# Two attention blocks with normalised queries and keys: score matmuls of two key heads on halves of the array's rows

## What is computed

```python
def _qk_norm(a):
    var = jnp.mean(jnp.square(a), axis=-1, keepdims=True)
    return a * jax.lax.rsqrt(var + EPS)

def _attn(xq, xkv, wq, wk, wv, wo, rep):
    q = jnp.einsum('btc,chd->bthd', xq, wq)      # 16 query heads of 64
    k = jnp.einsum('btc,chd->bthd', xkv, wk)     # 4 key heads of 64
    v = jnp.einsum('btc,chd->bthd', xkv, wv)
    q, k = (_qk_norm(q), _qk_norm(k))
    k = jnp.repeat(k, rep, axis=2)               # rep = 4
    v = jnp.repeat(v, rep, axis=2)
    logits = jnp.einsum('bqhd,bkhd->bhqk', q, k) * (1.0 / np.sqrt(64))
    attn = jax.nn.softmax(logits, axis=-1)
    out = jnp.einsum('bhqk,bkhd->bqhd', attn, v)
    return out.reshape(B, Tq, H * Dh) @ wo

x = _rmsnorm(latents, s1)
latents = latents + _attn(x, inputs, wq_c, wk_c, wv_c, wo_c, rep)   # block L2_ca
latents = latents + _swiglu_ffn(_rmsnorm(latents, s2), w1_1, w2_1)
z = _rmsnorm(latents, s3)
latents = latents + _attn(z, z, wq_s, wk_s, wv_s, wo_s, rep)        # block L2_sa
```

## Time and profile before

| what | value |
|---|---|
| median of 3 runs | 2165.87 us (2164.4 to 2177.83) |
| profiled execution, its own time | 2163.83 us |
| span of its trace, first to last instruction | 2162.0 us |
| mean granted TensorE clock | 0.921 of full |
| instructions | 34309 |

### The profile page before, as it was taken

How to read it: one execution, slowest core, us unless ns; L and a number is a source line. 1 busy time by engine, 2 the same in 40 slices (tenths; PEclk the granted TensorE clock), 3 DMA queues, 4 the chain that set the end, 5 groups by cost and what they waited for, 6 DMA issues and landing times.

```text
span 2162.0 us, 34309 instructions
## 1 busy us (share of the span) xinstructions
PE 1812.8 (84%) x10658; PEld 1289.2 (60%) x10658; DVE 1326.3 (61%) x3343; ACT 866.9 (40%) x2497; POOL 641.2 (30%) x710
## 2 busy tenths in 40 slices
PE   5969998389938689999869999695886969999888
PEld 4747775278837576776755554483443835555457
DVE  5856666111148765666757667595776956656555
ACT  4635554022216425555324444242331434545421
POOL 2325554200032334555500000040000415455433
PEclk9979998599969889999979999797998979999979
DMA  4000000378830000010100010101001000001100
GB/s 165 29 21 16 15 0 1 117 248 301 284 131 1 0 0 23 15 46 0 64 9 13 15 65 0 49 1 59 0 0 53 18 0 12 21 10 29 50 1 17
DMA packets 34247, 102.76 MB, mean 48 GB/s; under 512 B 2624, under 2 KB 25696, under 8 KB 26976
## 3 DMA queue, kind: packets, MB, share of 16 engines
q1 hardware_dynamic: 32608, 97.79, 13.1%
q0 software_dynamic: 1536, 3.67, 0.5%
HBM read 93.20 MB, written 8.26 MB: 47 GB/s over the span
## 4 chain that ended last, share of the span: by engine, by line
PE 55%; issue 15%; DVE 13%; POOL 8%; ACT 4%; DMA 3%; SPq 0%; POOLq 0%; DVEq 0%; ACTq 0%
PE ps L909 8%; PE ps L792 7%; POOL arena L1786 6%; PE ps L732 4%; PE ps L944 4%; PE ps L805 4%; PE ps L737 3%; PE ps L855 3%; PE ps L787 3%; PE ps L837 3%; PE ps L1039 2%; PE ps L1023 2%; DMA arena<-rows_hbm 2%; PE ps L832 2%; PE ps L724 2%
## 5 line engine op out<-in xcount | busy, mean ns | idle before, releaser
L1786 POOL TENSOR_TENSOR arena<-arena,rinv 112x375 f32<-112x375 f32 (+1 forms) x448 | 371.4, 829 | 524.5 <-DVE rinv L1460 513.6
L805 PEld LDWEIGHTS ps<-cst,arena 112*125 112x125 f32 (+1 forms) x1408 | 206.1, 182 | 182.5 <-POOL arena L1786 81.2
L792 PE MATMUL ps<-arena 128*112 128x112 f32 (+1 forms) x1024 | 277.3, 385 | 14.6 <-ACT arena L1148 13.0
L805 PE MATMUL ps<-cst,arena 112*125 112x112 f32 (+1 forms) x1408 | 237.7, 281 | 57.0 <-POOL arena L1786 56.7
L1148 ACT ACTIVATE arena<-ps,negmax 112x375 f32<-112x375 f32 (+1 forms) x384 | 190.5, 501 | 188.1 <-DVE negmax L1455 187.2
L1455 DVE TENSOR_REDUCE negmax<-ps 112x1 f32<-112x375 f32 (+1 forms) x288 | 159.4, 553 | 157.9 <-PE ps L792 157.6
L1834 POOL TENSOR_TENSOR w_split_sb<-wml,w_split_sb 128x512 fp32r<-128x512 f32 (+1 forms) x40 | 44.9, 1124 | 572.4 <-ACT w_split_sb L1197 570.5
L1469 DVE COPY arena<-ps 125x336 f32<-125x336 f32 x384 | 189.7, 494 | 12.0 <-PE ps L805 11.2
L909 PE MATMUL ps<-h_split_sb,w_split_sb 128*128 128x448 f32 x768 | 179.7, 384 | 8.4 <-DVE h_split_sb L1583 4.3
L1148 ACT ACTIVATE arena<-arena,negmax 112x112 f32<-112x112 f32 (+1 forms) x256 | 125.4, 491 | 140.6 <-DVE negmax L1444 109.0
L732 PE MATMUL ps<-wat,arena 128*125 128x256 f32 (+1 forms) x704 | 177.3, 390 | 2.5 <-ACT arena L1095 1.8
(11 more groups left out here) (202 smaller groups left out, 3063.1 us busy)
## 6 DMA issues: line engine op xcount, KB each, us to landing
wml<-in_wm_L_moe SPq DMA_DIRECT2D x21, 1028.0 KB, 5.8
wml<-in_wm_L_moe SPq DMA_DIRECT2D x21, 1024.0 KB, 6.3
craw<-in_ctx SPq DMA_DIRECT2D x40, 375.0 KB
wml<-in_wm_L_m SPq DMA_DIRECT2D x3, 3072.0 KB, 13.2
wat<-in_wa_L_ca SPq DMA_DIRECT2D x2, 2560.0 KB, 9.2
wml<-in_wm_L_m SPq DMA_DIRECT2D x2, 2048.0 KB, 9.5
rows_hbm<-wml SPq DMA_DIRECT2D x2, 1344.0 KB, 13.9
arena<-rows_hbm SPq DMA_DIRECT2D x21, 128.0 KB, 5.4
```

The lines of the kernel that those rows point to most:

```text
L792: last = mm(ps[0:S, blk.bank_at(s), i * blk.nk:(i + 1) * blk.nk], qz[:, parity(b), head_of(u) if blk.dh == 16 else u], kT[:, parity(b), u ...
L805: last = nc.tensor.transpose(ps[0:blk.kp, T_BANK + s % blk.t_banks, o:o + S], buf[:, i * blk.nk + q * blk.kp:i * blk.nk + (q + 1) * blk.kp ...
L1786: pool.tensor_tensor(p3, p3, r3, ALU.mult).then_inc(scaled, 1)
```

## The change

Both blocks are put into `PAIRS`. With that:

- Scores are made at even steps only, two units at a time, one for each of two key heads: each matmul has 64 rows (its own head's), so the zeros in `qz` are no longer read. The wait for a free score bank is for two banks ahead.
- The order of the units becomes head by head in pairs (`group_of`): heads 0 and 1 of chunk 0, of chunk 1, of chunk 2, then heads 2 and 3. `add_chunks` has its work at units 2 to 5 and 8 to 11 of a batch instead of 1, 2, 4, 5, 7, 8, 10, 11.
- QT0 and QT1 are copied out once each instead of twice, with scale 0.125 instead of the mask.

In `L2_sa` there are now four score banks (0 to 3) instead of two, so banks 2 and 3 are given up by pieces and output: pieces go to banks 7 and 5 in turn instead of 7, 5 and 2, and the output projection to bank 7 instead of 3. `project` of `L2_sa` therefore gets the wait for V0's copy (L850 to L852), and QT1 the wait for `update`.

```diff
     "L2_sa": ...
-        out_step=2, lag=1, s_banks=2, t_banks=2, w_banks=[7, 5, 2], out_bank=3),
+        out_step=2, lag=1, s_banks=4, t_banks=2, w_banks=[7, 5], out_bank=7),
...
-PAIRS = ("L3_ca",)
+PAIRS = ("L2_ca", "L2_sa", "L3_ca",)
```

## The result

Over 20 runs of each, the changed kernel takes 2176.27 us in the median (2172.55 to 2186.74), the kernel before 2170.14 us (2159.64 to 2177.83). The ratio is 1.0039, 95% interval 1.0027 to 1.0052: slower by about 8 us, where 4 us less were forecast, and above the forecast range. The profiled executions have spans of 2171.0 and 2162.0 us and mean granted clocks of 0.912 and 0.921. (The median of before is 4 us above that of the first three runs: executions of one kernel spread over some 18 us, and part of this is there before the stages of the change begin.

A forecast was written before the change was run, and what follows sets the result against it. DVE's chain, not PE alone, was taken to bound the periods. L2_ca's periods -2.1, its head and tail -1.5 and L2_sa -0.5 gave -4.1 us: 2159.7, or 2161.7 on the median, range 2147 to 2174.

The forecast's parts named there:

- L2_ca's periods: One batch of L2_ca from QT0 to the next: 30.68 us against 31.07, taken as 0.3 less, -2.1 over seven.
- QT0 to weigh: In L2_ca, weigh of heads 2 and 3 waits for DVE's last chunk addition and starts 0.84 us earlier.
- weigh to QP1: In L2_ca, pairs win 0.19 us, but project's wait for KP1's copy adds 0.64: 13.88 us against 13.43.
- QP1 to QT0: In L2_ca, DVE's chain behind QP1 keeps this at 10.70 us; PE waits about 1 us before QT0.
- PE is the bound throughout: Rival for L2_ca: all score savings count, 3.7 us per batch, about 32 with the head, time 2134; chance 0.10.
- L2_ca's head: Start of L2_ca: two fewer Q copies -0.8 us, and first-batch pair (0, 1) at the lower clock -1.1.
- L2_ca's tail: Last batch of L2_ca: one more DVE addition before weigh of heads 0 and 1, +0.6 us, less 0.2.
- unchanged, bounds -0.2 and +0.4: L2_sa's period from QT0 to QT0: DVE's list covers the savings and new waits, so no change.
- rival 2: Clock falls in L2_sa from more PE idle time: +9.8 us over seven periods, 2171.5 on the median; chance 0.14.
- The Trainium skill's rule on transposes: In L2_sa, transposes don't count as clock activity, so QT0 to KT0 is idle and every period falls: 2171.5.

The follow-up runs named there:

- runs with the fills: Extra unread full-row matmuls in idle heads and tails: L2_ca paired, QP0 moved 0.9937; the change plus one matmul per L2_sa batch 0.9873; kernel before 0.9932.
- half rows: Kernel before, with each L2_sa score matmul reading only its own head's 64 rows, order, banks, waits and columns kept: ratio 1.0068 to the kernel before.

## Why the prediction was wrong

- *L2_ca's periods*: right in mechanism and nearly in size. QT0 to weigh 6.00 us (6.1 said), weigh to QP1 14.10 (13.88), QP1 to QT0 10.77 (10.70), period 30.87 (30.68); the wait in front of QT0 0.96 (1). Project starts 1.60 us after KP1 (1.51), with 0.47 us of it idle by the profile. A pair takes 0.95 us to the next start (0.94). The 0.2 that weigh to QP1 was short of are its edges: KP0, KP1 and QP0 beside the pairs, and project behind its wait, take about 0.1 us longer each, where 0.09 per pair was counted. "PE is the bound throughout" would have won 30 us and is refuted.
- *L2_ca's head*: the first period is 2.3 us shorter, 1.1 and one period's 0.3 were said.
- *L2_ca's tail*: the step that put it at +0.4 failed. It is +3.8 us here, and between +1.1 and +3.7 in the other four runs with this order. I counted DVE's instructions and took PE's durations there as given; but PE idles longer (2.77 us ahead of project instead of 2.02), and project ran at 5.39 us instead of 3.71, in each of those runs. The runs with the fills bring these durations back to 3.71, so the clock is the cause of them. Part of the size is chance: of three runs with the tail unpaired two took 58.9 us, and one (half rows) 61.1, with project at 5.39 too, while the five paired ones took 60.0 to 62.7.
- *L2_sa, the period "unchanged, bounds -0.2 and +0.4"*: this is the step that made the prediction wrong. The waits and covers in it were right (19.35 us at full clock, weigh waiting 0.84 us for L1494). What was missing is the clock: the term put it at nothing, and six of seven periods had a fall, with 10.4 us more for the stage. The prediction had this as rival 2 with 0.14, priced at 9.8 us for a fall in every period. That the two numbers lie so near is luck: it counted 1.4 us per fall, for weigh and the sums alone, with the projections priced beside it at 1.5 more and left out of the sum, while the four falls of the last five periods cost 0.8, 3.9, 2.9 and 3.9 us against a period at full clock. In the longer ones the projections were slow too, as that remark allowed. Its likelihood was read from the idle time alone: the periods before stayed at full clock "with nearly as much idle". The half-row run shows that idle time alone was the wrong thing to compare: the matmuls that fill the rest had changed as well, and half-row matmuls in their place, with less idle time in the profile, were enough for the clock to fall.
- *The Trainium skill's rule on transposes* ("TensorE: Matmul & The Clock Gate", Part 4), by which the prediction had the fall come in every period, gave the right sign. The kernel before, with the same transposes, held full clock in five periods in a row, and no run here separates transposes from the rest; two of the changed kernel's last three periods with pieces had a fall and one had none, and one full-row matmul more was enough to keep the clock up.

## What to carry to other kernels

Where an engine's chain already bounds a stage, faster matmuls turn into idle time, and here idle time and half-row matmuls cost the clock, and with it several microseconds of work behind them at half speed: before pairing small contractions onto halves of the rows, look at the granted clock of the stretches that become thinner, not at the waits alone. Where the gain is hidden anyway, as in L2_sa, the matmuls on full rows with zeros were the faster choice (183.1 us against 203.3 with nothing else changed). Where TensorE has to wait, an extra full-row matmul into a free bank (0.75 us, nobody reads it) in the gap can pay many times over; here 57 of them, among some five thousand, gave more than the change was about. Such work belongs ahead of the wait: the extra pair that stood behind it was itself slow in each of the three falls.

## What the runs showed that was not expected

- Replacing full-row by half-row matmuls of the same columns, one by one and not in pairs, made the stage 20 us longer (203.3 against 183.1), with falls of the clock (0.79 in a period's window) and more busy time of PE (17.95 us in a period at full clock against 17.18).
- A lone half-row unit takes 0.93 us to the next start where a full-row unit takes 0.75: about 0.18 us more each time, and a pair (0.95 us) takes 0.20 more than one full-row unit. Whether what happens in this time or the number of rows is what lets the clock fall was not separated and stays open.
- A fall in a period of L2_sa costs 0.8 to 3.9 us in the changed kernel, 1.4 to 1.5 in the run with the pair issued twice and 4.4 in the half-row run. It is dear where it reaches the query projections (5.2 to 5.8 us instead of 3.7), since DVE's chain then starts later.
- Code that did not change is not free of falls: L2_sa as before had none, one or two of them in its last five periods, from run to run.
